# Router of the first three batches with the weight matrix held still and the tokens moving, in quarters of the array, logits transposed back

## The chip, the core and the metric

The kernel runs on one core of a Trainium2 chip. The core has a matrix engine (PE, TensorE; PEld is its weight load, which overlaps it), a vector engine (DVE), a scalar engine (ACT), GpSimd (POOL), a queue that only starts DMAs (SP), on-chip memory of 128 partitions (SBUF), and the accumulators into which PE writes (PSUM, 128 partitions in banks of 512 f32). Every engine works through its own list in order; semaphores join them. The metric is device microseconds of one execution: before the change 477.74 us, the median of three runs (477.26 to 477.96).

## The reference, cut to what matters

```
x = L0_attn_x                                # 4 batches x 512 tokens x 256 channels
h = layernorm(x) * (1 + ca) + sa
x = x + ga * attention(h)                    # 16 query heads, 4 key/value heads of 16
h = layernorm(x) * (1 + cb) + sb
probs = softmax(h @ router_w.T)              # router_w: 8 experts x 256 channels
w = the experts, best first, up to a sum of 0.9 of the probabilities
x = x + gb * sum over e of w[:, e] * (silu(h @ gate_w[e].T) * (h @ up_w[e].T)) @ down_w[e].T
```

The change concerns the product `h @ router_w.T` alone: 2048 tokens, 256 channels, 8 logits for each token.

## The kernel before

**Stages.** The four batches (b = 0 to 3) go through attention one after another, up to about 215 us; then comes the expert stage, in which tokens are gathered by lists, 256 at a time (an item), multiplied by one expert's three matrices, and added to the output by scattering DMAs. The attention of a batch is 16 steps, `gk` = 0 to 15. In each step PE computes two scores (units u = 2gk and 2gk + 1, L1537), ACT takes the exponents of each (L678), and PE multiplies them with v (`weigh_values`, L1639). The scores run one step ahead of the values. PSUM has room for two units of scores, so a score waits until ACT has read the unit two before it.

**What is woven in.** Between these steps stand the preparation of the next batch (its x is transposed by `turn_x` at gk = 0 and goes through the q, k, v projection at gk = 2 and 3) and the rest of the batch before (its attention output is projected, added to x, normalised to h, and h is transposed into `hT`, two tiles of 128 channels x 512 tokens). The places in the lists are written out by hand.

**The router.** `route(p)` computes the logits of batch p. It is called at the end (gk = 15) of batch 1 for p = 0, at the end of batch 2 for p = 1, at gk = 7 of batch 3 for p = 2, and among the first items of the expert stage for p = 3. For each of 4 token tiles and 2 channel tiles, the 128 x 128 block of `hT` is loaded as weight and the 8 columns of `w_r` move through: 8 matmuls in the program, for which the trace shows 16 weight loads and 16 matmuls, two passes for each f32 matmul. The result, tokens on the partitions, lies in bank 1 of psM as 4 x 8 columns.

**Who waits for the logits.** DVE copies them to SBUF (`take_logits`, L1027), finds the maximum and subtracts it (first lines of `stand_ahead`, L1126 and L1127), and goes on with comparisons that rank the experts. ACT takes the exponent of the difference (`exp_of_logits`, L709). On ACT this stands between two steps of the scores' exponents: behind step gk = 0 of batch 2 for p = 0, behind step 0 of batch 3 for p = 1, behind step 8 of batch 3 for p = 2. The exponents of the following step (L678) cannot start before it. For p = 2 DVE has in front of `take_logits` the split of a weight (`split_weight(0, 0, 0)`, L828).

**Where the next PE work stands.** After `route(0)` PE's list has the two scores of step 1 of batch 2, the values of step 0, and `turn_x(3)`. After `route(1)`: the scores of step 1 of batch 3, the values of step 0, and the transposes of the last y of batch 2 (`turn_y`). After `route(2)`: the scores of step 9 of batch 3, the values of step 8, and `turn_last_y(0, 1)`.

Of the kernel before, what the change touches and what calls it, by code (L numbers as in the profile page):

```python
# [30 lines left out]
def adaln_block(nc, x, wqT, wkT, wvT, woT, routerT, gateT, upT, downT, cT, wmod, out):  # L31
# [21 lines left out]
    YROWS = 32  # L53
    ROOT = 0.375
# [18 lines left out]
    with ctx:  # L73
# [75 lines left out]
        w_r = sb("w_r", [P, KC, E])  # L149
        mod_cols = sb("mod_cols", [P, 2, KC, B])  # L150
# [16 lines left out]
        squares = sb("squares", [P, QKV])  # L167
        norms = sb("norms", [P, TT, ALLH])
# [48 lines left out]
        for parts, part in ((w_hi, "w_hi"), (w_lo, "w_lo")):  # L217
# [25 lines left out]
         hT2_done, logit_ps, logit_done) = sems(  # L243
            "yT2_ps yT2_done w_gated o_ps x2_done bn_done ln_stats ln_eps ln_rstd h_scaled h_done h_out h_turned "
            "hT2_done logit_ps logit_done")
# [167 lines left out]
        def _(pool):  # L413
            pool.sem_inc(out_listed, 1)
            pool.memset(minus_half[:, :], -0.5).then_inc(zeroed, 1)
            pool.memset(ident[:, :], 0.0).then_inc(zeroed, 1)
            pool.wait_ge(zeroed, 2)
# [397 lines left out]
        def _(dve):  # L815
# [208 lines left out]

            def take_logits(p):
                dve.wait_ge(logit_ps, p + 1 + 3)
                dve.tensor_copy(logits[:, bass.ds(p * TT, TT), :],  # L1027
                                psM[:, 1, 0:TT * E].rearrange("p (t e) -> p t e", e=E)).then_inc(logit_done, 1)
# [28 lines left out]
            def body(b, parity, begin, end):  # L1057
# [9 lines left out]
                if end:  # L1067
                    take_sums(b - 1, G - 1)
                    if b >= 2:
                        take_logits(b - 2)  # L1070
                        stand_ahead(b - 2)
                    finish_y(b - 1, 1 - parity, G - 1)
                    if b >= 2:
                        choose_experts(b - 2)
                        routing_weights(b - 2)
# [28 lines left out]
                else:  # L1104
                    dve.wait_ge(gates_in, 16)
                    dve.wait_ge(wrest_in, 16 * (2 * R + 1))
                    gate_outputs(0)

# [97 lines left out]
            def last_body(parity):  # L1206

                p = LAST - 1
                take_sums(p, G - 1)
# [12 lines left out]
                split_weight(0, 0, 0)  # L1222
                take_logits(p)
# [206 lines left out]
        def _(pe):  # L1430
# [19 lines left out]
            def turn_x(n, first):  # L1450
                pe.wait_ge(xhat_done, (n + 1) * TT)
                if not first:
# [5 lines left out]
                    pe.wait_ge(logit_done, n)  # L1458
                for k in range(KC):
                    for tt in range(TT):  # L1460
                        mm = pe.transpose(psM[:, k, tt * P:(tt + 1) * P], xhat[:, tt, k * P:(k + 1) * P], ident[:, :])
                    mm.then_inc(xT_ps, 1)
# [134 lines left out]
            def route(p):  # L1597

                pe.wait_ge(hT2_done, (p + 3) * KC)
                for tt in range(TT):  # L1600
# [3 lines left out]
                mm.then_inc(logit_ps, 1)  # L1604

# [37 lines left out]
            def body(b, parity, begin, end):  # L1643
# [4 lines left out]
                for gk in range(G * TT):  # L1648
# [7 lines left out]
                    if gk == 0:  # L1656
                        turn_x(b + 1, False)
# [65 lines left out]
            def last_body(parity):  # L1723
                p = LAST - 1
                for gk in range(G * TT):
# [3 lines left out]
                    if gk == 2:  # L1729
                        turn_outputs(p, False)  # L1730
                    elif gk == 3:
# [153 lines left out]
```

## Time and profile before

| | |
|---|---|
| median of three runs | 477.74 us (477.26 to 477.96) |
| the profiled execution | 477.64 us, of which 476.0 us are the span of its instructions |
| PE busy | 437.6 us, 92% of the span |
| PE weight loads busy | 327.6 us, 69% |
| DVE busy | 330.4 us, 69% |
| ACT busy | 260.4 us, 55% |
| POOL busy | 196.4 us, 41% |
| mean granted TensorE clock | 0.993 |

The span is the time from the first to the last instruction; the rest of the execution, 1.64 us, lies around it. Busy shares are means over stages with different limits. A row of the timeline gives the start in microseconds, the length, the engine, the line, the operation with output and input, a count where several in a row are merged, and in brackets how long the engine had been idle and whose end it had waited for. The ends of matmuls are modelled.

### The profile page before, as it was taken

The numbers are of one execution on the slowest core, as the hardware profiler recorded it, in microseconds if no ns is written. First come the engines' busy times: TensorE is split into PE (matmuls) and PEld (weight loads), VectorE is DVE, ScalarE is ACT, GpSimd is POOL, SyncE is SP. The second block draws the span as 40 slices with busy tenths as digits, with TensorE's granted clock in tenths as the row PEclk, the third lists the DMA queues.
The fourth block names the chain that finished last, engine by engine and source line by source line (L and its number), as shares of the span: only waits on it lengthen the run. The fifth ranks groups of instructions, "written<-read, shape, count | busy, mean of one in ns | idle before, by whom it ended". The sixth has DMA issues, their size and how long they took to land. (4 is left out here: it accounts for less than half of the span.)

```text
span 476.0 us, 10007 instructions
## 1 busy us (share of the span) xinstructions
PE 437.6 (92%) x3466; PEld 327.6 (69%) x3466; DVE 330.4 (69%) x766; ACT 260.4 (55%) x380; POOL 196.4 (41%) x229
## 2 busy tenths in 40 slices
PE   6978888998999899999999899999999999999992
PEld 6443222442434344437999899999899999999992
DVE  3687885699579967689989768574566475756542
ACT  3277889768876888786341345353353353533330
POOL 4231023022002200011436566675766666776755
PEclk9999999999999999999999899999999999999998
DMA  8702307710011002044175358557538565554443
GB/s 252 246 1 48 88 1 77 102 45 0 2 48 44 1 1 90 4 134 134 49 226 119 70 124 225 134 110 181 114 67 211 86 180 129 121 92 106 80 79 45
DMA packets 30784, 46.00 MB, mean 97 GB/s; under 512 B 3588, under 2 KB 22276, under 8 KB 30728
## 3 DMA queue, kind: packets, MB, share of 16 engines
q0 software_dynamic: 11936, 22.50, 26.7%
q1 hardware_dynamic: 18792, 22.77, 14.8%
q8 instruction: 33, 0.54, 0.5%
q14 instruction: 23, 0.19, 0.1%
HBM read 34.44 MB, written 12.93 MB: 100 GB/s over the span
## 5 line engine op out<-in xcount | busy, mean ns | idle before, releaser
L678 ACT ACTIVATE probs<-psS 128x1024 f32<-128x1024 f32 x128 | 122.9, 1035 | 18.7 <-PE psS L1537 18.6
L1779 PE MATMUL psS<-hs_hi,w_hi 128*128 128x256 f32 x400 | 113.9, 285 | 3.6 <-DVE hs_lo L1297 2.1
L1779 PE MATMUL psS<-hs_lo,w_hi 128*128 128x256 f32 x400 | 113.1, 283 | 0.0
L1779 PE MATMUL psS<-hs_hi,w_lo 128*128 128x256 f32 x400 | 113.0, 283 | 0.0
L521 POOL DMA_INDIRECT out<-y_sel,idx_out x44 | 76.8, 1745 | 34.7 <-DVE y_sel L1337 20.8
L1779 PEld LDWEIGHTS psS<-hs_hi,w_hi 128*128 128x128 f32 x400 | 76.2, 190 | 5.1 <-issue 5.1
L1779 PEld LDWEIGHTS psS<-hs_lo,w_hi 128*128 128x128 f32 x400 | 76.0, 190 | 0.0
L1779 PEld LDWEIGHTS psS<-hs_hi,w_lo 128*128 128x128 f32 x400 | 76.0, 190 | 0.0
L507 POOL DMA_INDIRECT h_sel<-h_rows,idx_in x50 | 55.8, 1116 | 41.4 <-DVE sel L1303 17.6
L1639 PE MATMUL psY<-probs,v_aug 128*32 128x512 f32 x512 | 68.2, 605 | 0.0
L732 ACT ACTIVATE silu_g<-psS 128x512 f32<-128x512 f32 x50 | 29.9, 598 | 60.4 <-PE psS L1779 55.9
L1794 PE MATMUL psY<-w_hi,a_hi 128*128 128x256 f32 x196 | 57.4, 293 | 1.3 <-DVE a_lo L1315 1.3
L1315 DVE TENSOR_TENSOR a_lo<-a_full,a_hi 128x512 fp32r<-128x512 f32 x50 | 34.2, 687 | 34.7 <-ACT a_hi L737 22.4
L1794 PE MATMUL psY<-w_hi,a_lo 128*128 128x256 f32 x196 | 55.2, 282 | 0.0
L1794 PE MATMUL psY<-w_lo,a_hi 128*128 128x256 f32 x196 | 55.1, 281 | 0.0
L1537 PE MATMUL psS<-qT,kT 64*128 64x512 f16 x256 | 43.8, 384 | 9.9 <-ACT probs L678 8.1
L1310 DVE TENSOR_TENSOR a_full<-psS,silu_g 128x512 f32<-128x512 f32 x50 | 34.3, 686 | 25.6 <-PE psS L1779 22.3
L737 ACT CAST a_hi<-a_full 128x512 fp32r<-128x512 f32 x50 | 30.8, 622 | 36.9 <-PE psY L1794 32.0
L455 POOL COPY parted<-parted 128x512 f16<-128x512 f16 x14 | 9.6, 684 | 97.3 <-DVE parted L934 97.3
L1794 PEld LDWEIGHTS psY<-w_hi,a_hi 128*128 128x128 f32 x196 | 37.3, 190 | 1.7 <-DVE a_lo L1315 1.7
L1537 PEld LDWEIGHTS psS<-qT,kT 64*128 64x128 f16 x256 | 10.4, 93 | 39.3 <-ACT probs L678 25.8
L1794 PEld LDWEIGHTS psY<-w_lo,a_hi 128*128 128x128 f32 x196 | 37.2, 190 | 0.0
(229 smaller groups left out, 710.5 us busy)
## 6 DMA issues: line engine op xcount, KB each, us to landing
w_in<-gateT SPq DMA_DIRECT2D x8, 512.0 KB
w_in<-upT SPq DMA_DIRECT2D x8, 512.0 KB
w_in<-downT SPq DMA_DIRECT2D x8, 512.0 KB
h_rows<-h_nat SPq DMA_DIRECT2D x4, 528.0 KB
x_all<-x SPq DMA_DIRECT2D x4, 512.0 KB, 5.3
h_rows<-mod_table POOLq DMA_DIRECT2D x4, 512.0 KB
out<-x_all SPq DMA_DIRECT2D x4, 512.0 KB, 2.9
mod_rows<-mod_table SPq DMA_DIRECT2D x3, 512.0 KB, 6.2
```

Of the source, the lines that this page charges most:

```text
L455: pool.tensor_copy(q[:, :, 1:3, :], q[:, :, 0:4:3, :]).then_inc(parts_done, 1)
L507: pool.indirect_dma_start(h_sel[:, k, :], None, h_rows[0:rows, :], bass.IndirectOffsetOnAxis(ap=idx_in[:, k:k + 1], axis=0)).then_inc(gath ...
L521: pool.indirect_dma_start(out_rows[0:rows, :], bass.IndirectOffsetOnAxis(ap=idx_out[:, k:k + 1], axis=0), sums[:, k, :], None, compute_op= ...
L678: act.activation(probs[:, gk % 4, 2 * pair:2 * pair + 2, :], psS[:, pair, :, :], ACT.Exp, scale=ATT_SCALE / QK_UNIT ** 2).then_inc(probs_d ...
L732: act.activation(silu_g[:, h, :], psS[:, 0, h, :], ACT.Silu).then_inc(silu_ready, 1)
L737: act.copy(a_hi[:, 2 * h:2 * h + 2, :].rearrange("p i t -> p (i t)"), a_full[:, h, :]).then_inc(a_rounded, 1)
L1310: dve.tensor_tensor(a_full[:, h, :], psS[:, 1, h, :], silu_g[:, h, :], ALU.mult).then_inc(a_ready, 1)
L1315: dve.tensor_tensor(a_lo[:, 2 * h:2 * h + 2, :].rearrange("p i t -> p (i t)"), a_full[:, h, :], a_hi[:, 2 * h:2 * h + 2, :].rearrange("p i ...
L1537: mm = pe.matmul(psS[:, u % 2, j, :], kT[rows, parity, g // 2, kt * P:(kt + 1) * P], qT[rows, parity, 2 * g + pair, :], start=True, stop=True)
L1639: mm = pe.matmul(psY[r * YROWS:(r + 1) * YROWS, g % 2, :], v_aug[:, parity, kt, 2 * (g // 2) + r % 2, :], probs[:, gk % 4, r, :], start=kt ...
L1779: mm = pe.matmul(ps[:, i * SW:(i + 1) * SW], w, v[:, k, :], start=at == 0, stop=at == 3 * KC - 1)
L1794: mm = pe.matmul(down_rows(j, last), v[:, i, tok], w, start=i == 0 and n == 0, stop=i == KI - 1 and n == 2)
```

## The change

For p = 0, 1, 2 the roles of the two operands are exchanged. `w_rw` is the router's matrix widened with zeros from 8 to 32 columns: GpSimd clears it once, DVE copies the 8 columns into it once, at the end of batch 0. `route` then holds a 128 x 32 block of it as weight and moves 128 tokens of `hT` through. Token tile tt writes the 32 partitions from 32tt on of one PSUM bank, so the four tiles use four column quarters of the array. The logits now lie with experts on the partitions and tokens along the row. DVE copies them out (`take_turned_logits`, 128 x 128), PE transposes them once (`turn_logits`), and `take_logits` picks the first 8 of each 32 columns. `logits_t` is the first 128 columns of the buffer `squares`. The last batch keeps the old form. In `turn_x` the wait for `logit_done` moves from before the first channel tile to before the second, which alone writes the bank of the logits.

```diff
+    LROWS = P // TT
...
+        w_rw = sb("w_rw", [P, KC, LROWS])
...
+        logits_t = squares[:, 0:P]
...
+            pool.memset(w_rw[:, :, :], 0.0).then_inc(w_widened, 1)
...
+            def take_turned_logits(p):
+
+                dve.wait_ge(logit_ps, p + 1 + 3)
+                dve.tensor_copy(logits_t, psM[:, 1, 0:P]).then_inc(logit_t_done, 1)
+
             def take_logits(p):
+                if p < LAST:
+                    dve.wait_ge(logit_back, p + 1)
+                    dve.tensor_copy(logits[:, bass.ds(p * TT, TT), :],
+                                    psM[:, 1, P:2 * P].rearrange("p (t r) -> p t r", r=LROWS)[:, :, 0:E]).then_inc(logit_done, 1)
+                    return
...
                 if end:
+                    if b >= 2:
+                        take_turned_logits(b - 2)
                     take_sums(b - 1, G - 1)
...
+                    dve.wait_ge(w_widened, 1)
+                    dve.tensor_copy(w_rw[:, :, 0:E], w_r[:, :, :]).then_inc(w_widened, 1)
...
                 p = LAST - 1
+                take_turned_logits(p - 1)
                 take_sums(p, G - 1)
...
                 split_weight(0, 0, 0)
+                take_turned_logits(p)
                 take_logits(p)
...
             def turn_x(n, first):
-                    pe.wait_ge(logit_done, n)
                 for k in range(KC):
+                    if k and not first:
+                        pe.wait_ge(logit_done, n)
...
             def route(p):
                 pe.wait_ge(hT2_done, (p + 3) * KC)
+                if p < LAST:
+
+                    pe.wait_ge(w_widened, 2)
+                    for k in range(KC):
+                        for tt in range(TT):
+                            mm = pe.matmul(psM[tt * LROWS:(tt + 1) * LROWS, 1, 0:P], w_rw[:, k, :], hT[:, k, tt * P:(tt + 1) * P],
+                                           start=k == 0, stop=k == KC - 1)
+                    mm.then_inc(logit_ps, 1)
+                    return
...
+            def turn_logits(p):
+                pe.wait_ge(logit_t_done, p + 1)
+                pe.transpose(psM[:, 1, P:2 * P], logits_t, ident[:, :]).then_inc(logit_back, 1)
...
                     weigh_values(b, parity, gk)
                     if gk == 0:
+                        if b >= 2:
+                            turn_logits(b - 2)
                         turn_x(b + 1, False)
...
-                    if gk == 2:
+                    if gk == 0:
+                        turn_logits(p - 1)
+                    elif gk == 2:
                         turn_outputs(p, False)
+                    elif gk == 8:
+                        turn_logits(p)
```

On PE, from the end of batch 1 into batch 2, the first of the three places, the list before is this (`w_r,hT` is the router, `qT,kT` the scores, `probs,v_aug` the values, `ident,xhat` the transposes of x):

```order
L1602 MATMUL psM<-w_r,hT 128x8 [waits hT2_done]
L1602 MATMUL psM<-w_r,hT 128x8 x7
L1537 MATMUL psS<-qT,kT 128x512 [waits probs_done,v_copied]
L1537 MATMUL psS<-qT,kT 128x512
L1537 MATMUL psS<-qT,kT 128x512 [waits probs_done]
L1537 MATMUL psS<-qT,kT 128x512
L1639 MATMUL psY<-probs,v_aug 32x512 [waits probs_done,y_sb]
L1639 MATMUL psY<-probs,v_aug 32x512 x3
L1461 MATMUL psM<-ident,xhat 128x128 [waits trk_done,tr_done,yn_done,logit_done,hT2_done,xhat_done]
L1461 MATMUL psM<-ident,xhat 128x128 x7
```

and with the change this, where `hT,w_rw` is the router and `ident,squares` the transpose of the logits:

```order
L1627 MATMUL psM<-hT,w_rw 32x128 [waits w_widened,hT2_done]
L1627 MATMUL psM<-hT,w_rw 32x128 x7
L1559 MATMUL psS<-qT,kT 128x512 [waits probs_done,v_copied]
L1559 MATMUL psS<-qT,kT 128x512
L1559 MATMUL psS<-qT,kT 128x512 [waits probs_done]
L1559 MATMUL psS<-qT,kT 128x512
L1674 MATMUL psY<-probs,v_aug 32x512 [waits probs_done,y_sb]
L1674 MATMUL psY<-probs,v_aug 32x512 x3
L1639 MATMUL psM<-ident,squares 128x128 [waits logit_t_done]
L1483 MATMUL psM<-ident,xhat 128x128 [waits trk_done,yn_done,tr_done,hT2_done,xhat_done]
L1483 MATMUL psM<-ident,xhat 128x128 x3
L1483 MATMUL psM<-ident,xhat 128x128 [waits logit_done]
```

The router keeps its place. The transpose of the logits stands behind the scores of step 1 and behind the values of step 0, and the second half of the transposes of x waits for the copied logits.

On PE in batch 3, at the third place, steps 7 to 9, before:

```order
L1602 MATMUL psM<-w_r,hT 128x8 [waits hT2_done]
L1602 MATMUL psM<-w_r,hT 128x8 x7
L1537 MATMUL psS<-qT,kT 128x512 [waits probs_done]
L1537 MATMUL psS<-qT,kT 128x512
L1537 MATMUL psS<-qT,kT 128x512 [waits probs_done]
L1537 MATMUL psS<-qT,kT 128x512
L1639 MATMUL psY<-probs,v_aug 32x512 [waits probs_done,y_sb]
L1639 MATMUL psY<-probs,v_aug 32x512 x3
L1688 MATMUL psM<-ident,yT 128x128 [waits logit_done,y_sb]
```

and with the change (`ident,yT` are the transposes of the last batch's y):

```order
L1627 MATMUL psM<-hT,w_rw 32x128 [waits w_widened,hT2_done]
L1627 MATMUL psM<-hT,w_rw 32x128 x7
L1559 MATMUL psS<-qT,kT 128x512 [waits probs_done]
L1559 MATMUL psS<-qT,kT 128x512
L1559 MATMUL psS<-qT,kT 128x512 [waits probs_done]
L1559 MATMUL psS<-qT,kT 128x512
L1639 MATMUL psM<-ident,squares 128x128 [waits logit_t_done]
L1674 MATMUL psY<-probs,v_aug 32x512 [waits probs_done,y_sb]
L1674 MATMUL psY<-probs,v_aug 32x512 x3
L1725 MATMUL psM<-ident,yT 128x128 [waits logit_done,y_sb]
```

Here the transpose of the logits stands behind the scores but ahead of the values. The second place, at the start of batch 3, has the same order as the third.

On DVE at the first place, before, from the normalised x of batch 3 (`xhat`) to the subtraction of the maximum (`rt_p`):

```order
L900 TENSOR_SCALAR xhat<-x_all,mean_var,rstd 128x256 [waits ln1_rstd]
L900 TENSOR_SCALAR xhat<-x_all,mean_var,rstd 128x256 x3
L952 COPY yT<-psY 128x512 [waits pv_done]
L1027 COPY logits<-psM 128x32 [waits logit_ps]
L1126 TENSOR_REDUCE rt_max<-logits 128x4 [waits logit_done,consts]
L1127 TENSOR_TENSOR rt_p<-logits,rt_max 128x32 [waits rt_step]
```

and with the change (`squares` is the buffer of the turned logits):

```order
L905 TENSOR_SCALAR xhat<-x_all,mean_var,rstd 128x256 [waits ln1_rstd]
L905 TENSOR_SCALAR xhat<-x_all,mean_var,rstd 128x256 x3
L1033 COPY squares<-psM 128x128 [waits logit_ps]
L957 COPY yT<-psY 128x512 [waits pv_done]
L1038 COPY logits<-psM 128x32 [waits logit_back]
L1145 TENSOR_REDUCE rt_max<-logits 128x4 [waits logit_done,consts]
L1146 TENSOR_TENSOR rt_p<-logits,rt_max 128x32 [waits rt_step]
```

DVE now waits for the router ahead of the copy of the sums (`yT`), and for the transpose behind it.

## Rows read from the trace of the kernel before

**Rows 1.** Busy times in two stretches: length, PE, PEld, DVE, ACT, POOL, clock, DMA

```profile
120.00:165.00 45.00, 41.44 (x291) 17.77 (x289) 36.98 (x108) 33.98 (x47) 5.73 (x13) 1.00 0.07 25
300.00:476.00 176.00, 164.68 (x1404) 163.47 (x1403) 99.55 (x161) 66.25 (x105) 115.31 (x110) 0.99 0.55 114
```

**Rows 2.** Timeline, first place, from batch 1 into batch 2

```profile
123.15 1.95 ACT L678 ACTIVATE probs<-psS 128x1024 f32<-128x1024 f32 x2
...
124.09 1.95 PE L1602 MATMUL psM<-w_r,hT 128*128 128x8 f32 x16
...
125.97 0.60 PE L1537 MATMUL psS<-qT,kT 64*128 64x512 f16 x4
126.08 0.19 DVE L1027 COPY logits<-psM 128x32 f32<-128x32 f32 x1 [0.60 <-PE psM L1602]
...
126.51 1.06 PE L1639 MATMUL psY<-probs,v_aug 128*32 128x512 f32 x8
...
126.82 0.23 ACT L709 ACTIVATE rt_p<-rt_p 128x32 f32<-128x32 f32 x1 [1.73 <-DVE rt_p L1127]
126.95 1.92 ACT L678 ACTIVATE probs<-psS 128x1024 f32<-128x1024 f32 x2
...
127.51 1.09 PE L1461 MATMUL psM<-ident,xhat 128*128 128x128 f32 x8
...
128.92 0.10 PEld L1537 LDWEIGHTS psS<-qT,kT 64*128 64x128 f16 x2 [0.30 <-ACT probs L678]
129.25 0.16 PEld L1639 LDWEIGHTS psY<-probs,v_aug 128*32 128x32 f32 x8 [0.23 <-issue]
...
132.09 0.10 PEld L1537 LDWEIGHTS psS<-qT,kT 64*128 64x128 f16 x2 [0.82 <-ACT probs L678]
```

**Rows 3.** Timeline in two narrower windows: the two passes of one step's values

```profile
123.09 0.64 PE L1639 MATMUL psY<-probs,v_aug 128*32 128x512 f32 x4
...
123.55 0.61 PE L1639 MATMUL psY<-probs,v_aug 128*32 128x512 f32 x4
```

**Rows 4.** A timeline row, then two groups by line: busy us, mean ns

```profile
112.03 0.62 PE L1509 MATMUL psM<-ident_h,parted 128*128 128x128 f16 x8
...
L1561 PE MATMUL psM<-ident,yT 128*128 128x128 f32 x23 | 3.7, 284 | 1.3 <-DVE yT L952 1.3
...
L952 DVE COPY yT<-psY 128x512 f32<-128x512 f32 x9 | 6.2, 685 | 0.9 <-PE psY L1639 0.9
```

**Rows 5.** Timeline, second place (start of batch 3), 171 to 178 us

```profile
172.03 1.95 ACT L678 ACTIVATE probs<-psS 128x1024 f32<-128x1024 f32 x2
...
172.98 1.95 PE L1602 MATMUL psM<-w_r,hT 128*128 128x8 f32 x16
...
174.97 0.19 DVE L1027 COPY logits<-psM 128x32 f32<-128x32 f32 x1 [1.16 <-PE psM L1602]
...
177.82 0.10 PEld L1537 LDWEIGHTS psS<-qT,kT 64*128 64x128 f16 x2 [0.74 <-ACT probs L678]
```

**Rows 6.** Timeline, third place (batch 3, step 8), 194 to 198 us

```profile
194.20 1.94 ACT L678 ACTIVATE probs<-psS 128x1024 f32<-128x1024 f32 x2 [0.92 <-PE psS L1537]
...
194.65 1.22 DVE L828 TENSOR_TENSOR w_lo<-w_in,w_hi 128x1024 fp32r<-128x1024 f32 x1
195.30 1.95 PE L1602 MATMUL psM<-w_r,hT 128*128 128x8 f32 x16
...
197.29 0.19 DVE L1027 COPY logits<-psM 128x32 f32<-128x32 f32 x1 [1.43 <-PE psM L1602]
```

**Rows 7.** Timeline, batch 0 into 1: normalised x, and its transposes on PE

```profile
76.83 1.38 DVE L900 TENSOR_SCALAR xhat<-x_all,mean_var,rstd 128x256 f32<-128x256 f32 x4
...
79.09 1.09 PE L1461 MATMUL psM<-ident,xhat 128*128 128x128 f32 x8
```

**Rows 8.** Busy times, columns as rows 1: two stretches of the expert stage

```profile
250.00:255.00 5.00, 5.00 (x51) 4.96 (x50) 5.00 (x9) 1.77 (x4) 2.04 (x3) 1.00 0.42 60
264.00:268.00 4.00, 4.00 (x22) 4.00 (x23) 3.97 (x7) 0.60 (x1) 2.89 (x4) 0.57 0.21 67
```

More of the change, by code:

```diff
@@ L242, in adaln_block @@
         (yT2_ps, yT2_done, w_gated, o_ps, x2_done, bn_done, ln_stats, ln_eps, ln_rstd, h_scaled, h_done, h_out, h_turned,
-         hT2_done, logit_ps, logit_done) = sems(
+         hT2_done, w_widened, logit_ps, logit_t_done, logit_back, logit_done) = sems(
             "yT2_ps yT2_done w_gated o_ps x2_done bn_done ln_stats ln_eps ln_rstd h_scaled h_done h_out h_turned "
-            "hT2_done logit_ps logit_done")
+            "hT2_done w_widened logit_ps logit_t_done logit_back logit_done")
         (rt_step, rt_diff, rt_exp, rt_kept, w_kept, rank_ps, lists0_ps, listed0, one_done, lists_ps, idx_ready,
```

## The prediction

> **What bounds the kernel now.** I read the busy times by stretch first. In the attention of batch 2 PE is busy 41.4 of 45 us and ACT 34.0 of 45; in the expert stage PE is busy 164.7 of 176 us [rows 1]. So in the expert stage the end moves with PE's start into it, and before it PE and ACT share the bound: whoever is late makes the other late. Which of the two decides at the three places of the router has to be read from the timeline.
>
> At each of the three places the same chain stands. The router takes PE from 124.09 to 125.97, 1.88 us for 16 passes; DVE copies the logits at 126.08, takes the maximum, subtracts it, and ACT, idle for 1.73 us, takes their exponent at 126.82 and only then goes on with the scores' exponents at 126.95 [rows 2]. PE then waits for ACT in turn, 0.30 us before the weight load at 128.92 and 0.82 us before that at 132.09 [rows 2], and again before 177.82, 0.74 us [rows 5]. So right behind the router the path runs router, DVE, the exponent of the logits on ACT, the exponents of the scores, the next score on PE. What counts is not PE's time in the router but the moment at which DVE has the logits in the old layout: 126.08, 174.97 and 197.29 [rows 2, 5, 6]. Whatever moves these moves the path.
>
> **What is removed and what comes in.** Removed at each of three places: 1.88 us of PE. In its place: 8 matmuls of 128 moving columns on 32 weight columns, 16 passes in four quarters. The form is in the trace: the values of one step are 8 passes of 512 columns on 128*32 tiles, and the second four start 0.46 us after the first four (123.09 and 123.55) [rows 3]. So four quarters run together; 128 columns take a quarter of that, 0.115 us, and four rounds take 0.46 us. This is the lower end. The upper end with packing comes from short matmuls that hold PE by their number: 8 of 128 columns in 0.62 us, 0.078 each [rows 4], so 16 take 1.24 us. I take 0.46, since rows 3 are the same form and type.
>
> Then DVE copies 128x128 out of PSUM. No such copy is in the trace; 128x32 takes 0.19 [rows 2] and 128x512 takes 0.685 [rows 4], so it lies between, by columns at 0.29, which I take. Then one transpose on PE: a single one lasts 0.284 [rows 4] and holds PE for 1.09/8 = 0.14 [rows 2]. From its start to DVE's next copy I take 0.36: 0.28, some 0.04 to get going and the 0.04 between the router's end (124.09 + 1.95 = 126.04) and DVE's start at 126.08 [rows 2]. The last copy is as wide as before, 0.19.
>
> Chain alone: 0.46 + 0.17 (end of the last matmul) + 0.04 + 0.29 + 0.05 + 0.36 = 1.37 us against 1.99 from 124.09 to 126.08. If nothing stood between, each place would gain 0.6 us. But the transpose stands in PE's list behind other work, and this decides.
>
> First place. After the router (124.55) come the two scores of step 1. The second waits for ACT's second exponent, which ends at 123.15 + 1.95 = 125.10; a score follows ACT's end by 0.05 (126.95 + 1.92 = 128.87, load at 128.92), and what follows a score does so by 0.33 (128.92 to 129.25) [rows 2]. So the values of step 0 start at 125.48. They hold PE 1.00 us (126.51 to 127.51) [rows 2], and the transpose starts at 126.48, DVE's last copy at 126.84. Before, it was 126.08: **0.76 us later**. ACT waits until 127.58 instead of 126.82, and its next two exponents end at 129.63 instead of 128.87. PE is early by then with the transposes of x, but it waits for ACT both at the next score and at the one at 132.09, where it had waited before [rows 2]; the delay passes to PE whole, and the projection that follows is PE's own. The moved wait in `turn_x` costs nothing, as the logits are there when the first half is done.
>
> Second place. The transpose stands behind the scores and ahead of the values. ACT's second exponent ends at 172.03 + 1.95 = 173.98 [rows 5], so the last score starts at 174.03, the transpose at 174.36, DVE's copy at 174.72, against 174.97: **0.25 us earlier**. DVE's first copy is done by 173.93 and the copy of the sums behind it by about 174.6, so neither is late.
>
> Third place. ACT's exponent ends at 194.20 + 1.94 = 196.14, the last score starts at 196.19, the transpose at 196.52, DVE's copy at 196.88, against 197.29 [rows 6]: **0.41 us earlier**. DVE's split of a weight ends at 195.87 [rows 6], just before the router's result at 195.96, so it costs nothing; the first copy ends at 196.25.
>
> Between the second and third place, and behind the third up to the first items, the work hangs on this chain or on PE, which here does not lose time of its own, so both gains pass on.
>
> Set-up: the copy into the widened weight is as wide as a copy of 0.19 or less and stands before the normalised x of batch 2, which ends at 78.21 while PE comes for it at 79.09 [rows 7]. Cover 0.88 us, cost nothing. The clearing on POOL stands while it waits for its previous clearing; nothing.
>
> Sum: +0.76 - 0.25 - 0.41 = +0.10 us. On the profiled execution of 477.64 us that is 477.74; on the median of 477.74 it is **477.8 us**. If the 128x128 copy took 0.685, the second place would gain only 0.02 and the third 0.23, and the sum would be +0.5.
>
> The Trainium skill, "TensorEngine Tiling (Array Packing)", PSUM Bottleneck, says that tiling makes TensorE faster but not the evacuation, and that the PSUM copy may become the bottleneck. The rows agree in kind: DVE's added copy and ACT's wait are what is left of 1.42 us saved. But copies alone would still leave the chain shorter by 0.6; it is the place in PE's list that takes the gain at the first place, and of that the page says nothing.
>
> **Rivals.**
> Slow packing (the other side): the sixteen short passes are held at 0.078 each. The router then takes 1.24 us; scores start at 125.33, the values 0.54 later (125.97 to 126.51 [rows 2]), and the transpose gives the logits at 127.23, +1.15. Second place +0.3 (DVE's two copies come late), third +0.15. Sum +1.6: 479.3 us. It decides as soon as a router takes more than about 0.8 us. For it: matmuls with few columns do pay by number in rows 4. Against it: in rows 3 four tiles start together.
> No packing (the change does not do what it says): the router takes 1.88 us as before and the added steps come on top. At the first place scores, values and transpose put the logits at 125.97 + 0.54 + 1.00 + 0.36 = 127.87, +1.8; at the others scores and transpose give +0.8 each; +3.4: 481.1 us. Against it stand rows 3.
> The delay of the first place is absorbed in batch 2: the sum is -0.66, 477.1 us. For it: PE idles 3.6 us in that stretch [rows 1]. Against it: those waits are for ACT, and ACT is what is late.
> PE's saved time reaches the end: 3 x (1.88 - 0.46 - 0.14) = 3.8 us, 473.9 us. For it: PE is 92% busy there. Against it: ACT's idle 1.73 us ends with DVE, not with PE.
> The clock: in one stretch of the expert stage the granted clock is 0.57, mostly the lower level of 1.2 GHz, and 4 us hold 22 matmuls where 5 us at 2.4 GHz hold 51 [rows 8]; that costs 4 - 22 x 0.098 = 1.8 us. It begins after an idle gap of PE. Were this gap to fall otherwise, the time would be 476.0; were a second one to arise in PE's new idle time near 128 us, about 479.6.
>
> **How the numbers follow.** Forecast, as summed: 0.50. Slow packing 0.13, no packing 0.08, absorbed 0.12, PE's time reaches the end 0.06, clock drop gone 0.05, a second one 0.06. About 0.2%, 0.96 us, is what a measurement of this kernel can tell from no change. Faster holds the last-but-two and the clock drop gone and a little of the forecast's edge: 0.12. Slower holds both packing rivals and the second drop, 0.27, a little less for a mild slow packing: 0.26. The rest, 0.62, is the forecast and the absorbed delay. The range of 8 in 10 leaves out no packing, PE's time and the clock drop gone: 476.9 to 479.4 us.
>
> **What would show it.** Right: the router's 16 passes within 0.5 to 0.6 us; DVE's copy of the logits 0.6 to 0.9 us later than before, relative to the values of batch 1's last step, at the first place, and 0.2 to 0.5 us earlier at the other two; ACT's idle time before L709's exponent grown from 1.73 to about 2.5 us, then shrunk to about 1.4 and 1.5; PE's idle time near 128 us. Wrong: the router at over 0.8 us, DVE's first copy at over 0.4, or the projection of batch 3 (after 133 us) not starting later by about 0.75.

## The result, and the profile of the changed kernel

The changed kernel takes 479.81 us (median of 20 runs, 478.13 to 482.08), the kernel before 477.93 us beside it (20 runs, 476.41 to 480.55): ratio 1.0037, 95% interval 1.0022 to 1.0052. It is slower, by 1.8 us; forecast were 477.8 us and at most 479.4.

**The three places.** They came out nearly as worked out. The timeline of the changed kernel around the first place (start, duration, engine, line, operation, output and input, count, idle time before and what ended it), answering to [rows 2] and [rows 3]:

```profile
124.17 1.06 PE L1674 MATMUL psY<-probs,v_aug 128*32 128x512 f32 x8
125.05 0.62 PE L1627 MATMUL psM<-hT,w_rw 128*32 128x128 f32 x16
125.60 0.39 PE L1559 MATMUL psS<-qT,kT 64*128 64x512 f16 x2
...
126.54 1.07 PE L1674 MATMUL psY<-probs,v_aug 128*32 128x512 f32 x8
127.54 0.33 PE L1639 MATMUL psM<-ident,squares 128*128 128x128 f32 x1
...
125.87 0.28 DVE L1033 COPY squares<-psM 128x128 f32<-128x128 f32 x1
127.90 0.19 DVE L1038 COPY logits<-psM 128x32 f32<-128x32 f32 x1 [1.15 <-PE psM L1639]
...
128.64 0.23 ACT L714 ACTIVATE rt_p<-rt_p 128x32 f32<-128x32 f32 x1 [2.48 <-DVE rt_p L1146]
...
129.83 0.10 PEld L1559 LDWEIGHTS psS<-qT,kT 64*128 64x128 f16 x2 [1.27 <-ACT probs L683]
130.75 0.10 PEld L1559 LDWEIGHTS psS<-qT,kT 64*128 64x128 f16 x2 [0.82 <-ACT probs L683]
```

The router holds PE from 125.05, where its first matmul starts, to 125.60, where the next score starts: 0.55 us (taken: 0.46). The copy of 128x128 takes 0.28 (0.29). The logits are there at 127.90, 3.73 us after the start of the step's values at 124.17; before, it was 126.08 after 123.09, so 2.99: 0.74 us later (0.76). ACT's wait grew from 1.73 to 2.48, and PE waits 1.27 us for ACT where it had waited 0.30. At the second and third place the transpose stands ahead of the values. Before, the last values ahead of the router started here:

```profile
171.98 1.06 PE L1639 MATMUL psY<-probs,v_aug 128*32 128x512 f32 x8
...
194.31 1.07 PE L1639 MATMUL psY<-probs,v_aug 128*32 128x512 f32 x8
```

and with the change:

```profile
173.80 1.06 PE L1674 MATMUL psY<-probs,v_aug 128*32 128x512 f32 x8
...
176.54 0.19 DVE L1038 COPY logits<-psM 128x32 f32<-128x32 f32 x1 [0.28 <-PE psM L1639]
...
177.28 0.23 ACT L714 ACTIVATE rt_p<-rt_p 128x32 f32<-128x32 f32 x1 [1.48 <-DVE rt_p L1146]
...
195.88 1.07 PE L1674 MATMUL psY<-probs,v_aug 128*32 128x512 f32 x8
196.76 0.62 PE L1627 MATMUL psM<-hT,w_rw 128*32 128x128 f32 x16
...
198.46 0.19 DVE L1038 COPY logits<-psM 128x32 f32<-128x32 f32 x1 [0.72 <-PE psM L1639]
```

From the start of these values to the logits it is 176.54 - 173.80 = 2.74 us at the second place, before 174.97 - 171.98 = 2.99: 0.25 us earlier (forecast 0.25). At the third it is 198.46 - 195.88 = 2.58, before 197.29 - 194.31 = 2.98: 0.40 earlier (0.41). Of the 0.40 us, 0.29 lie between the router's start and the logits (1.70 us in place of 1.99 [rows 6]), the rest between the values and the router.

**The stretches.** The same view as [rows 1] and [rows 8]; columns are length, PE, PEld, DVE, ACT, POOL (busy, count), granted clock, DMA share, GB/s:

```profile
120.00:165.00 45.00, 40.51 (x289) 16.38 (x281) 35.36 (x105) 33.83 (x47) 6.60 (x14) 1.00 0.07 25
300.00:476.00 176.00, 167.74 (x1426) 166.18 (x1424) 101.73 (x165) 66.60 (x106) 113.21 (x111) 1.00 0.56 117
...
11.20:14.60 3.40, 3.00 (x9) 1.79 (x8) 0.00 (x0) 1.27 (x2) 3.24 (x1) 0.50 1.09 336
209.20:212.50 3.30, 3.30 (x15) 0.80 (x15) 3.11 (x9) 1.94 (x2) 1.31 (x2) 0.50 0.56 134
```

No second drop of the clock came near 128 us: it is 1.00 from 120 to 165. But this execution had two stretches at the lower level (granted 0.50, so 1.2 GHz) that the profile of before had at 1.00, and its 480.86 us can't be compared with 477.64 us as it stands. The drops change from run to run in both kernels, as the next section shows.

### The profile page after: what moved, and what is told of

Read it like the earlier page. It is cut to its first block and busy times, and to the rows that moved or that the text cites. A ratio compares the mean times of both kernels' runs of the same rounds, so it can differ in the third digit from the quotient of the medians.

```text
span 479.2 us, 10018 instructions
## 1 busy us (share of the span) xinstructions
PE 439.0 (92%) x3469; PEld 326.4 (68%) x3469; DVE 331.5 (69%) x770; ACT 260.3 (54%) x380; POOL 193.2 (40%) x230
## 5 line engine op out<-in xcount | busy, mean ns | idle before, releaser
L526 POOL DMA_INDIRECT out<-y_sel,idx_out x44 | 75.6, 1719 | 35.7 <-DVE y_sel L1358 22.6
L512 POOL DMA_INDIRECT h_sel<-h_rows,idx_in x50 | 54.0, 1081 | 43.5 <-DVE sel L1324 18.7
```

Of the source, the lines that this page charges most:

```text
L512: pool.indirect_dma_start(h_sel[:, k, :], None, h_rows[0:rows, :], bass.IndirectOffsetOnAxis(ap=idx_in[:, k:k + 1], axis=0)).then_inc(gath ...
L526: pool.indirect_dma_start(out_rows[0:rows, :], bass.IndirectOffsetOnAxis(ap=idx_out[:, k:k + 1], axis=0), sums[:, k, :], None, compute_op= ...
```

## How runs were compared

Two profiles show the change well only when their clock drops agree. The second profiles of both kernels (aa_before and aa_after below) have them at nearly the same places, 3.4 us long each, from 10.1 and 9.1 us on in the set-up and from 266.1 and 265.1 us on in the expert stage. I matched PE's matmuls of the two one by one and took the difference of their start times, after less before:

```
start in aa_before   difference   what lies between
   118.8              -0.55
   135.2              +0.19       first place: +0.74
   184.0              -0.06       second place: -0.25
   200.9              -0.48       third place: -0.42
   305.7              -0.35       lists, batch 3's output, items 0 to 8: +0.13
   313.7              +0.86       item 9: +1.21
   402.2              +0.85
   410.3              +1.59       item 19: +0.74
   466.8              +1.57
```

So the three places give +0.07 us, where +0.10 was forecast, and 1.95 us are lost in two items of the expert stage, of which the prediction said nothing. (The last decimal depends on which matmuls are matched.) An item is one pass of the walk over the experts: 256 gathered rows of h, turned on PE (the transposes that read `h_sel`), multiplied by up, gate and down weights, scattered to the output.

For the median of many runs I use each run's mean granted clock too. Over the timed runs of this study (391, without one of 819.71 us), each kernel about its own mean, a run is 292 us longer per unit of mean clock, that is 1.05 us for one stretch of 3.4 us at half clock. "At equal clock" below is the mean time brought to a clock of 0.990 by that slope; kernels with 12 runs have a standard error of 0.13 to 0.34 us. The six sets of runs of the kernel before lie between 478.11 and 478.47 there, mean 478.3.

One slope for all is rough, beyond that error. A low-clock stretch near 265 us makes items 1 to 8 take 77.1 to 77.4 us in place of 76.2 to 76.3 in most profiles, but only 76.5 in the two of before_short. And the last stretch at the lower level, 2.5 to 5.5 us long within the span, counts in the mean clock and costs nothing: from item 25 on every profile takes 15.8 to 16.0 us. So differences of some tenths "at equal clock" show nothing by themselves.

## Experiments

**The same kernels again.** No edit. 

> The kernel before, timed against itself, to see how far its time and its mean granted clock scatter from run to run. Both theories: same, ratio within 0.2% of 1. Theory C (the change makes the clock fall to 1.2 GHz more often): the mean clock over the runs lies near 0.992, one fall and the end of the span, clearly above the 0.988 to 0.989 of the changed kernel. Rival M (a mechanism in the work itself costs the missing 1.7 us): the mean clock here is the same 0.988 to 0.989 as with the change, and the times at equal clock are 1.7 us lower.

> The changed kernel again, beside the kernel before on the same chip. Theory C: +1 to +2.5 us, with a mean clock lower than that of the kernel before by 0.003 to 0.004 (one fall of 3.4 us at half clock is 0.0036 of the span), and at equal clock within 0.4 us of it. Rival M: +1 to +2.5 us at equal clock. Chance (the 20 runs lay apart by the scatter of the clock alone): +0.1 us, as the three places sum.

Measured: 478.36 and 479.66 us; at equal clock 478.5 and 479.3. The first comparison gives 1.1 us at equal clock (479.4 against 478.3), this pair 0.8. Theory C of these two expectations (the clock falls more often) explains at most a part: the mean clock is 0.9875 with the change against 0.9898, worth 0.7 us by the slope, and sets of the kernel before went as low as 0.9874. The waits of PE in the expert stage, 300 to 345 us, that aa_before does not have (engine, tile, line, released by: us in total, times, longest):

```profile
PEld psM L1804 <- DMA h_sel<-h_rows,idx_in: 1.2, 1, 1.2
PE psM L1804 <- DMA h_sel<-h_rows,idx_in: 1.0, 1, 1.0
```

**The turn back ahead of the values at the first place.** 

> The change with one instruction moved: at the first place the transpose of the logits stands ahead of the values of step 0, as it does at the other two. My sum for the place: the copy of the logits 1.00 us earlier than with the change, so 0.25 us earlier than before instead of 0.75 later. The trace must show the PE work from batch 2 on 1.0 us earlier than with the change, and the three places then sum to -0.9 us against before. In the time: 1.0 us less than the changed kernel beside it if the clock falls equally often; against the kernel before -0.9 us where the clock plays no part (chance), +0.7 us if the 1.7 us beyond my sum come with the short router itself (C or M), and as low as -0.9 us if PE's idle time at the first place was what brought the clock down.

```
                     if gk == 0 and b >= 2:
+                        turn_logits(b - 2)
                     weigh_values(b, parity, gk)
                     if gk == 0:
-                        if b >= 2:
-                            turn_logits(b - 2)
```

Its timeline at the first place:

```profile
126.15 0.19 DVE L1038 COPY logits<-psM 128x32 f32<-128x32 f32 x1 [0.16 <-PE psM L1639]
126.89 0.23 ACT L714 ACTIVATE rt_p<-rt_p 128x32 f32<-128x32 f32 x1 [1.48 <-DVE rt_p L1146]
```

The values start at 123.41, so the logits come 2.74 us later, 0.25 us earlier than before: the place in PE's list was what cost 1 us there. PE is 0.95 us ahead of before at 204 us. Yet the time is 478.80 us, ratio 1.0007 (0.9979 to 1.0035), at equal clock 478.3, that of before. So at equal clock 1 us is lost behind 204 us again.

**Only some places in the new form.** `TURNED` is the tuple of batches whose router is in the new form:

```
-                if p < LAST:
+                if p in TURNED:
```

> The new form for batch 0's logits alone (first place), the old form at the other two. By the sum +0.75 us against before, and the trace shows +0.75 us behind the first place and no further step at 175 and 197 us. Rival, that the first place also makes the clock fall (PE idles there for 1.3 us): +2.4 us, and a mean clock lower by 0.0036 than before.

> The new form for the routers of batches 1 and 2 only (second and third place); the router of batch 0, at the first place, as before. By the sum of the prediction: -0.25 and -0.41, the projection behind the third place 0.66 us earlier than before, and 477.4 us against 478.06, ratio 0.9986. Theory A (the gains of these places are lost behind 204 us, in waits for the gathered rows of the items): by 204 us the same 0.66 us ahead, but the end about 0.4 us later than before, 478.5, with PE's waits for h_sel in the expert stage of 1 to 2 us in place of 0 to 1. Theory B (the loss is one of the first place, carried on): 477.4 us.

> The new form for the router of batch 1 only (second place). By the sum: 0.25 us earlier from there on, 477.8 us. Theory A with its cause at the third place: the same, 477.8. Theory A with its cause anywhere in an earlier or later phase of the items: 478.1 to 478.9.

> The new form for the router of batch 2 only (third place). By the sum: 0.41 us earlier from there on, 477.65 us. Theory A with its cause at the third place: about 1.1 us lost behind 204 us, so 478.7, with waits for h_sel of 1 to 2 us.

> All three routers as before; of the change only the widened weight (its tile of 512 bytes a partition, its clearing on POOL and its copy on DVE) and the wait moved inside turn_x remain. The prediction and theories A and B: 478.06 us, ratio 1.000. Theory C (the loss behind 204 us comes from the new tile, that is from where the later tiles lie, or from the set-up): about 1.1 us later, 479.2.

Measured: place1_only 478.70 us (ratio 1.0012, 0.999 to 1.0033), places23_only 479.43 (1.0009, 0.9988 to 1.003), p2_only 477.63 (0.9985, 0.9961 to 1.0009), p3_only 478.63 (0.999, 0.9967 to 1.0014), none_turned 477.46 (0.9973, 0.9953 to 0.9993). By the shift of PE each place gave what it was to give: p2_only -0.26 us at 183 us, p3_only -0.42 at 204, places23_only -0.26 and -0.41. At equal clock the first place costs 0.7 (forecast 0.76), the second gains 0.15 (0.25), the third 0.5 (0.41), each with an error of 0.2 to 0.3; of the ratios only that of none_turned leaves out 1. Theory B falls, and so does the theory C of these runs (the new tile or the set-up), since none_turned is not slower. (The tile has 256 bytes a partition, 2 x 32 f32, not 512.) But the second and third together are, at equal clock, 0.7 us slower than before in place of 0.66 us faster: theory A holds for the two together and for neither alone. That a term is lost only in company pointed away from the places themselves.

**The wait at item 9.** POOL's timeline in aa_before, the scatters and gathers around item 9:

```profile
298.44 0.18 POOL L513 COPY idx_out<-idx_all 128x2 int32 x1 [0.98 <-DMA out<-y_sel,idx_out]
300.29 1.62 POOL L521 DMA_INDIRECT out<-y_sel,idx_out  x1 [1.66 <-DVE y_sel L1337]
302.21 1.58 POOL L521 DMA_INDIRECT out<-y_sel,idx_out  x1 [0.30 <-issue]
303.23 0.77 POOL L496 COPY idx_in<-idx_all 128x2 int32 x1
304.80 1.05 POOL L507 DMA_INDIRECT h_sel<-h_rows,idx_in  x1 [0.79 <-issue]
```

and in aa_after, where PE is 0.35 us ahead up to here:

```profile
298.75 0.18 POOL L518 COPY idx_out<-idx_all 128x2 int32 x1 [1.62 <-DMA out<-y_sel,idx_out]
300.59 1.62 POOL L526 DMA_INDIRECT out<-y_sel,idx_out  x1 [1.66 <-DVE y_sel L1358]
302.51 1.58 POOL L526 DMA_INDIRECT out<-y_sel,idx_out  x1 [0.30 <-PE psM L1804]
303.53 0.77 POOL L501 COPY idx_in<-idx_all 128x2 int32 x1
305.10 1.04 POOL L512 DMA_INDIRECT h_sel<-h_rows,idx_in  x1 [0.79 <-issue]
```

The scatter of an earlier item lands late (POOL idles 1.62 us for it, not 0.98), DVE may write `y_sel` only then, POOL's next two scatters wait for DVE, and the gather of item 9 stands behind them in POOL's list: 3.30 us behind item 8's transposes in place of 2.64, so 0.66 us late. PE's own timeline, aa_before first:

```profile
311.11 0.60 PE L1763 MATMUL psM<-ident,h_sel 128*128 128x128 f32 x4
```

```profile
311.94 0.42 PEld L1804 LDWEIGHTS psM<-ident,h_sel 128*128 128x128 f32 x4 [1.23 <-DMA h_sel<-h_rows,idx_in]
311.94 0.66 PE L1804 MATMUL psM<-ident,h_sel 128*128 128x128 f32 x4 [1.02 <-DMA h_sel<-h_rows,idx_in]
```

These 0.66 us alone would not have made PE wait. DVE waits for the same rows (all of them, from both gathers of the item), aa_before first:

```profile
309.79 0.43 DVE L1303 TENSOR_SCALAR sel<-h_sel 128x528 f32 x1 [0.62 <-DMA h_sel<-h_rows,idx_in]
```

```profile
312.10 0.43 DVE L1324 TENSOR_SCALAR sel<-h_sel 128x528 f32 x1 [3.29 <-DMA h_sel<-h_rows,idx_in]
```

In aa_before the rows were there at 309.8, 1.2 us before PE loads them at 311.00. In aa_after they came 2.3 us later. Each gather leaves up to 16 landing marks in the trace (some are missing). In aa_after the last but one of item 9 is at 309.95 and the last at 311.89; had it come with the others, PE would have had the rows 0.8 us before it needed them.

What is in the way? The trace has every DMA packet with its queue, and q8 carries instructions in pieces of 16 KB. In aa_after one such piece starts 5.5 us ahead of item 8's transposes, beside the scatters and gathers, in the half microsecond from 296.2:

```profile
q0 software_dynamic: 70, 0.07, 91.2%
q1 hardware_dynamic: 33, 0.05, 25.3%
q8 instruction: 1, 0.02, 13.7%
```

In the same half microsecond by item 8, from 296.6, aa_before has none; its piece starts 4.9 us ahead:

```profile
q0 software_dynamic: 87, 0.10, 124.7%
q1 hardware_dynamic: 17, 0.02, 11.8%
```

(Columns: packets, MB, their time as a share of the 16 engines in the window.) Each piece lasts 0.9 to 2.0 us, as one packet on one DMA engine. In all 19 profiles this piece and POOL's chain go together, counted from item 8's transposes: piece at -5.30 to -5.49 us and next copy of `idx_out` on POOL at -2.86 to -3.06 (7 profiles), or piece at -4.57 to -4.93 and copy at -3.52 to -4.10 (12 profiles). Of the seven, six have a wait for gathered rows of 0.31 to 1.43 us on PE's weight load at item 9; of the twelve, none. At item 19, counted from its own transposes: piece at -2.4 to -2.8 us, wait 0.8 to 1.4 us (8 profiles); elsewhere, wait at most 0.7.

The late landing goes with the next piece, the one that comes while item 9's own rows are under way. Behind the issue of the second gather of item 9 it starts at 1.6 to 2.4 us in six profiles (2.3 in aa_after), and there the last landing is 0.8 to 2.0 us behind the last but one; in the other 13 it starts at 3.0 us or later (3.0 in aa_before), and the last landing is at most 0.2 us behind. The six are those in which PE waits. It is so over all 26 items of all 19 profiles, if the bounds are set by these rows: with a piece 1.4 to 2.45 us behind the second gather, one landing is late by 0.3 us or more in 66 of 77 cases; with no piece from 1.5 us ahead of it to 6 us behind, in 9 of 164. And the place of the piece goes with the length of PE's list. At item 9 it starts 5.0 to 5.8 us behind the gather with eight instructions fewer on PE than before, 3.0 to 5.0 with two or three fewer, 2.4 to 3.3 with as many, 2.0 with three more, and 1.6 to 2.3 with six more.

**Longer lists of instructions.** If the fetches matter, then what the change adds elsewhere in the code can shift them. Six increments of a semaphore on PE, or four on DVE, that nobody waits for, in the kernel before:

```
+            for n in range(6):
+                pe.sem_inc(passed, 1)
             turn_x(0, True)
```

> The kernel before, with six more instructions on PE alone (increments of a semaphore that nobody waits for), issued at about 9 us in its wait for xhat: as many as the change adds there in all. Every profile with the new form at both the second and the third place (four of four) had DVE's y_sel at 2.7 to 3.1 us before the ninth gathered item, a fetch of 16 KB of instructions at -5.3 to -5.5 us and PE waiting 0.4 to 1.3 us for that item; no other profile (none of six) had it: y_sel at -3.0 to -4.0, the fetch at -4.6 to -4.9, no wait. Theory F, with PE's list as the one whose length moves the fetch: fetch at -5.3, the wait at item 9, and 479.1 us against 478.1 (at equal clock). Theory F with DVE's list: as before, 478.1. Theory W (the weights and rows arrive in another phase because PE itself is 0.66 us early): as before, 478.1.

> The kernel before, with four more instructions on DVE alone (increments of a semaphore that nobody waits for), issued at about 1.5 us in its first wait: as many as the change adds there. Theory F with DVE's list: the fetch at -5.3 us before item 9, y_sel at -2.8, PE's wait of 0.4 to 1.3 us there and 479.1 us at equal clock against 478.1. Theory F with PE's list, and theory W: as before, 478.1.

> dve_longer once more. Theory F (the wait costs what it lasts, whenever the profile has it): the wait at item 9 in this profile too and 479.1 us at the usual clock (before 478.3). If the wait is there again and the time is again that of before, the wait is given back elsewhere; if it is not there, it comes and goes with the run.

Both kernels got the early piece (-5.48, -5.32) and the late copy of `idx_out` (-3.06, -2.86), and PE waited 0.70 and 1.43 us at item 9. pe_longer: 478.83 us, at equal clock 479.0, 0.7 us above before (its ratio, 1.0006, 0.9988 to 1.0025, does not tell it from before by itself). dve_longer: 479.07, at equal clock 478.3, nothing. dve_again: 477.82 us, 478.2; it had the early piece too (-5.49), but PE's wait at item 9 was 0. So the wait arises in the kernel before too, with no edit at the router, and it comes and goes from run to run of one kernel: the next piece started 2.4 us behind item 9's second gather in dve_longer and 3.1 us in dve_again. DVE's four instructions cost nothing that the timed runs show.

**Shorter lists.** Four of the 28 idle transposes with which PE starts (eight instructions) are left out, `stay_awake(24)` for `stay_awake(28)`; after_refilled also has eight increments on DVE.

> The kernel after, with four of the 28 idle transposes left out that PE does from 1.7 us on (each a weight load and a matmul on PE, their results are used by nobody): the change's eleven added instructions less eight, so three more than before, as in the kernels that never showed the wait. Theory F (what the change adds behind its own sum comes from the length of the code, which moves the fetches of instructions against the scatters and gathers of the items; six profiles of kernels with four or more added show it, six with three or less don't): the fetch 4.6 to 4.9 us before item 9's predecessor, y_sel at -3.0 to -4.0, no wait for item 9, and 478.4 us at the usual clock, 0.1 above before, in place of 479.4. Theory W (both places early by 0.66 us bring it about, whatever the length): the wait of 0.4 to 1.3 us at item 9 stays and the time is 479.4 us. A longer low-clock stretch in the set-up can add up to 1 us to either; it would show before 20 us.

> The kernel turn_first (the turn back ahead of the values at the first place), with four of the 28 idle transposes left out likewise. Theory F: no wait at item 9, the 0.95 us by which it is ahead at 204 us reaches the end: 477.35 us at the usual clock against 478.3 before. Theory W: 478.3, as turn_first.

> The kernel after with the four idle transposes left out and eight increments of an unused semaphore added on DVE, issued in its first wait: the length is that of after again. Theory F (the length of the code): the wait at item 9 is back, y_sel at -2.8 us, the fetch at -5.3, and about 0.9 us over after_short: 478.8 us at the usual clock. Theory T (the four transposes left out are what helped): no wait, 477.9 us, as after_short.

> The kernel before with the four idle transposes left out (eight instructions fewer). It never had the wait at item 9, so theory F: no wait there, and 478.2 us at the usual clock, as before, unless the shorter code brings a fetch to another place. Theory T: 477.2 us.

> before_short once more. Theory F: the time of before, ratio 1.000. Theory T (the four idle transposes left out gain by themselves): ratio 0.9985 or less.

> turn_first_short once more. Theory F: 477.3 us, ratio 0.998 against before; by chance alone the ratio would be nearer to 1.000 this time.

Measured: after_short 479.34 us (1.0015, 0.9997 to 1.0034; one of its 12 runs took 819.71 us and is left out of means), turn_first_short 477.30 (0.9979, 0.9959 to 0.9999), again 477.47 (0.9972, 0.995 to 0.9994), after_refilled 478.87 (1.0015, 0.9991 to 1.0039), before_short 478.23 (0.9988, 0.9966 to 1.0009), again 478.65 (1.0005, 0.9985 to 1.0026). None of the six has the wait at item 9 (after_refilled has the longest of all at item 19, 1.4 us). POOL in turn_first_short, where PE is 1.8 us ahead of aa_before, 0.95 by its places and most of the rest because its profile has no low-clock stretch near 265 us:

```profile
296.46 0.18 POOL L518 COPY idx_out<-idx_all 128x2 int32 x1 [0.56 <-issue]
298.31 1.62 POOL L526 DMA_INDIRECT out<-y_sel,idx_out  x1 [1.66 <-DVE y_sel L1358]
...
302.81 1.04 POOL L512 DMA_INDIRECT h_sel<-h_rows,idx_in  x1 [0.79 <-issue]
```

It is 302.81 - 300.37 = 2.44 us behind item 8 with the gather, aa_before 2.64, aa_after 3.30. **turn_first_short is faster than both kernels**, twice, by 1.1 and 1.0 us against before in the medians; both intervals end just short of 1. Against the two runs of before_short, which has the same transposes left out, it is faster by 478.42 - 477.34 = 1.08 us in the means, where its places give 0.95; but at equal clock by 0.2 only (477.2 and 477.4), so this comparison depends on how the clock is counted. Behind the set-up, from the first score to the end, its two profiles take 441.5 us and those of before_short 442.6 and 442.7, of which their low-clock stretch is about 0.25. For the changed kernel itself the gain of the shorter list is less plain: by their ratios, both 1.0015, after_short and after_refilled are still 0.7 us above before, and only at equal clock are they below it (by 0.5 and 0.2), while their profiles have 6.8 us at the lower level in the set-up and their first score 1.8 us later than in before. Theory T falls for the time as measured: before_short is not faster than before, though both intervals leave room for 0.7 us. At equal clock it looks 0.8 to 1.0 us faster; some of this is its cheap stretch near 262 us (above), and some can be real, for its two profiles lose 0.1 us each in the items' waits, those of before 1.1 and 0.4. after_refilled refutes the simplest form of theory F, that only the sum of instructions over engines counts.

**All kernels together.** "Sum" is what the places give (PE's shift up to 204 us), "rest" the time at equal clock less 478.3 less the sum. "Items" is, in the profile, the time from item 8 to 10 plus that from 18 to 20, above the 17.72 + 18.00 us that they take without a wait.

```
kernel              PE's list   sum     rest   items
before, aa_before      0         0      0, +0.2   1.1, 0.4
none_turned           -3         0     -0.4    0.6
place1_only            0       +0.76    0.0    0.1
p2_only                0       -0.25   +0.1    0.4
p3_only                0       -0.41   -0.1    0.9
pe_longer             +6         0     +0.7    1.5
places23_only         +3       -0.66   +1.3    2.3
after, aa_after       +6       +0.10   +1.0, +0.9   1.6, 2.4
turn_first            +6       -0.95   +1.0    1.6
dve_longer, again      0         0      0, -0.1   1.9, 1.1
after_refilled        -2       +0.10   -0.3    1.4
after_short           -2       +0.10   -0.6    0.3
turn_first_short, again  -2    -0.95   -0.1, -0.1   0.2, 0.2
before_short, again   -8         0     -0.8, -1.0   0.1, 0.1
```

("PE's list" counts PE's executed instructions in the profile against before.) Every kernel with three or more instructions added on PE has 0.7 to 1.3 us left over and 1.5 to 2.4 us in the two stretches; no other kernel has over 0.2 us left over. The profile of a kernel is one run, and DVE's kernels show that its waits need not be those of the timed runs.

The profiles by themselves close the account, run by run, and need no slope. Take the time from the first score of batch 0 to the end of the span; subtract what the places give, the "items", and what items 1 to 8 take above 76.24 us (the low-clock stretch near 265 us). In the 15 profiles that have no low-clock stretch between 30 and 260 us, 441.7 to 442.4 us are left, with and without the change. So behind the set-up nothing but the places, these waits and the clock makes one profile longer than another, and in dve_longer too the wait was paid in full.

## Why the prediction was wrong

- *The router 0.46, the copy 0.29, the transpose 0.36 us:* 0.55, 0.28 and 127.90 - 127.54 = 0.36. The router was taken 0.09 too small, the others are right. No packing and slow packing fall.
- *The first place 0.76 later, the second 0.25 and the third 0.41 earlier:* 0.74, 0.25 and 0.42 by PE's shift. The shifts of PE in place1_only, p2_only and p3_only confirm each, turn_first that the place in PE's list makes the first one. The router's missing 0.09 did not count at the first place, where ACT's exponents release the score behind it, as the prediction has it.
- *The delay passes to PE whole; PE's saved time does not reach the end:* right.
- *No drop of the clock in PE's new idle time:* right, 1.00. But I took the clock's stretches [rows 8] as fixed. They are not: before has none in the set-up in one profile and one of 3.4 us in the other, and its runs spread from 476.1 to 482.8 us; the mean clock accounts for about half of that variance.
- *The set-up costs nothing:* right in its own terms, none_turned is not slower.
- **The failed step:** "in the expert stage the end moves with PE's start into it", so that the sum could stop at the third place and both gains pass on. The forecast had no term behind 204 us. There the changed kernel loses 1.0 us at equal clock, and 1.95 us in the matched profiles, in waits for gathered rows at items 9 and 19. At item 9 the rows were there 1.2 us before PE needed them in aa_before; in aa_after POOL issued them 0.66 us later, and one landing came 1.9 us behind all others, with a piece of instructions under way on the DMA engines. The profile of before showed that these waits were near: between 290 and 425 us PE's weight loads wait for `h_sel` once, 1.1 us, and DVE waits for it five times, 6.7 us in all. I had looked only for what the change does to PE, DVE and ACT at its three places.

Shown by runs: that the loss is not at the places; that it is in those waits in the profiles, where the account closes without any other term; that lengthening PE's list alone brings about 0.7 us of it at equal clock; and that turn_first gains 1.3 us or more by a shorter list (478.80 against 477.30 and 477.47). Shown as going together, over 494 items: the piece of instructions and the late landing. Not shown: that the two share one DMA engine, as the trace does not name the engine; why the scatter ahead of item 8 lands late; and how often the timed runs have the waits. Open too are the remaining 0.6 to 0.7 us of the measured 1.8, part of which is a lower mean clock of the changed kernel's runs (0.9885 and 0.9875, the six sets of before 0.9874 to 0.9900) that I can't tell from chance. That the three places came out within 0.03 us in sum was no luck, as each was right by itself; but the sum was not the time.

## What to carry to other kernels

A chain of small steps can be costed well from the timeline, if each step is put at its place in its engine's list; the costly error is to end the sum where the edit ends. Look behind it for waits that occur already or whose margin is about a microsecond (here PE's and DVE's for gathered rows) and take them into the range, for any edit, also one that only adds instructions. And where a kernel is tuned to such margins, a control that adds a few idle instructions to the kernel before tells more than a second look at the edit.

## What the runs showed of the hardware

- Sixteen passes of 128 columns on 128*32 tiles in four quarters (f32) take 0.55 us, 0.034 each, beside 0.078 for the short full-width f16 passes of [rows 4].
- Instruction fetches share the DMA engines with data. Each piece on q8 took 0.9 to 2.0 us of one engine; a kernel with some 10000 executed instructions has 33. The Trainium skill, "Runtime: NRT & Kernel Launch", Instruction fetch mechanics, says that instructions are streamed in 16 KB blocks and that crossing a block is mostly hidden. The size agrees with the trace. Whether an engine stood still for its own instructions was not measured here; but a piece 1.4 to 2.45 us behind the issue of a gather goes with one late landing of its rows (66 of 77 cases in 19 profiles, against 9 of 164 without a piece near), and at items 9 and 19 such a landing made PE wait up to 1.4 us.
- The granted clock of one kernel differs from run to run: its mean over one execution was 0.983 to 0.997 in the kernel before. A stretch of 3.4 us at the lower level cost 0.8 to 1.2 us near 265 us in most kernels, 0.3 in before_short, and at the very end nothing.
